# Clipping the attention scores on VectorE instead of GpSimd in a graph network kernel

## The chip, the cores and the metric

The kernel runs on one core of a Trainium2 chip. The metric is the time of one execution on the device in microseconds, the median of several runs. The core's engines are TensorE (PE in the profile), VectorE (DVE), ScalarE (ACT), GpSimd (POOL) and SyncE (SP), each with its own instruction stream; semaphores order them against each other.

## What is computed

Four graph layers over 6250 nodes of 96 features and 100000 edges sorted by destination. The change touches the first layer, an attention along the edges with four heads:

```python
q = (embeds[rows] @ qW).reshape(e, HEADS, dh)
k = (embeds[cols] @ kW).reshape(e, HEADS, dh)
v = (embeds[cols] @ vW).reshape(e, HEADS, dh)
scores = jnp.clip(jnp.einsum('ehd,ehd->eh', q, k), -10.0, 10.0)
exp_s = jnp.exp(scores)
norms = jax.ops.segment_sum(exp_s, rows, num_segments=nvar)[rows]
w = exp_s / (norms + 1e-08)
res = jax.ops.segment_sum(w[:, :, None] * v, rows, num_segments=nvar).reshape(nvar, d)
```

The other three (a softmax aggregation, ten steps of propagation, two graph convolutions) come behind it and are left as they are.

## The kernel before

Edges are first put in slots: one cell for each pair of a tile of 128 source nodes (49 tiles) and a group of 256 destination nodes (25 groups). The attention stage then goes over the source tiles, and within a tile over five **chunks** of five groups; a chunk holds 5 x 128 edge slots. There are 49 x 5 = 245 chunks. In the names below `X` is a pair of tiles and `e` a chunk in it.

No row is gathered by an address. VectorE builds one-hot matrices and TensorE multiplies by them. For a chunk:

- `turn_source` (L995) and `turn_destination` (L1000, twice) compare the slots' node numbers with the partition number: the one-hots `hT`, three planes of 640 in float16. TensorE uses them as weights to fetch the queries (`query`, L1117, into PSUM bank `pq`) and the keys and values (`take`, L1105, into banks `pk`). ScalarE copies the latter to SBUF in three pieces (`copy_kv`, L1180, into `kvs`).
- `score` (L981) multiplies queries, read from PSUM, by keys, and `score_sum` (L988) adds over the 24 features of a head: 128 x 20 scores `sc`.
- `clip` (L1057) bounds them by two values held per partition in `bound`.
- `exponent` (L1166, ScalarE) writes the exponentials into the weight columns of `wv`.
- `weigh` (L1062, GpSimd) multiplies the values by them, 128 x 480, also into `wv`.
- `total` (L1127, TensorE) sums `wv` by source node with the one-hots `hs` (`one_hots`, L1024, float32, 128 x 640).
- `one_hots` also makes `hd` (L1029, bfloat16, 128 x 768), by destination; `build` (L1141) multiplies it by `hs` to get the dense adjacency blocks that the later layers use, and `evacuate` (L1159) copies these out.

The order is written by hand. Each engine has a step function, called for c = 0, 1, 2, ...; within it each piece of work is for chunk c minus a fixed lag. On VectorE a step is `score` of chunk c-2, `turn_source` of c, `score_sum` of c-2, `turn_destination` of c, every fifth step `factors` (L1008 to L1019: a cast and three small products from which `hd` is made), `one_hots` of c, and once in five steps the reciprocal L1035. On GpSimd a step is `clip` and `weigh` of chunk c-2, and once in five steps `denominate` (L1071) or `normalize` (L1076 to L1080). On TensorE it is `take` and `query` of c-1, `build` of c-1 and `total` of c-3. On ScalarE it is `copy_kv` of c-1, once in five `copy_sums`, `exponent` of c-2, `evacuate` of c-1. The texts below name a step by c modulo 5: step 0 is the one with `factors`, step 4 the one that ends with the reciprocal.

Most buffers are double (`hT`, `kvs`, `qk`, `sc`, `wv`, `hd`), `rows` and `hs` have five.

## Time and profile before

| | |
|---|---|
| median of 3 runs | 4195.71 us (4194.11 to 4196.58) |
| profiled execution, own time | 4197.43 us |
| its span | 4196.1 us |
| mean granted TensorE clock | 0.981 |
| busy: TensorE, VectorE, ScalarE, GpSimd | 3913.7, 1912.2, 1301.4, 574.5 us |
| L1057, the clip on GpSimd, 245 of them | 251.2 us busy |
| L1062, `weigh`, 245 | 248.3 us busy |
| L1024, `hs`, 245 | 237.4 us busy |

The span is 4196.1 us, in which the attention stage lies between about 280 and 1235 us. A timeline row gives the start of an instruction from the span's start, its length, the engine, the line, the operation, what it writes and reads (with partitions x elements and type), and how many neighbouring ones the row merges. In brackets stands how long the engine had been idle and what ended that. Starts on VectorE can be closer than the lengths: the end of one instruction overlaps the start of the next.

### The profile page before, as it was taken

To read this page: it belongs to the slowest core of one execution; us is meant where nothing else is said; L and a number is where in the kernel's file an instruction comes from. 1 tells how busy PE (TensorE), PEld (TensorE's weight loads), DVE (VectorE), ACT (ScalarE), POOL (GpSimd) and SP (SyncE) were. 2 spreads that over 40 slices of the span, in tenths; PEclk is the share of its full clock that TensorE was granted. 3 is DMA by queue.
4 is the path that set the end of the run, shared out by engine and by line. 5 is a ranking of instruction groups with operands and counts; after the bars stand their busy time and mean duration, and the time that the engine had idled before them with its cause. 6 is when DMAs were issued, how large, how long until landed. Compare 5 with 4: busy or idle time off the path is not lost.

```text
span 4196.1 us, 126663 instructions
## 1 busy us (share of the span) xinstructions
PE 3913.7 (93%) x46212; PEld 3676.0 (88%) x46212; DVE 1912.2 (46%) x4409; ACT 1301.4 (31%) x4246; POOL 574.5 (14%) x708
## 2 busy tenths in 40 slices
PE   3779999999979999899999999999999999979898
PEld 2668999999965556899999999999999999979898
DVE  8989999999984332322222222222222222251211
ACT  1236666666653000222222222222222222220100
POOL 1015565555540000000000000000000000000000
PEclk9989999999989999999999999999999999989999
DMA  1029889898883331566665556666666565556574
GB/s 39 3 69 212 212 212 213 210 211 212 211 222 97 113 108 54 198 203 203 203 203 203 203 203 203 203 203 203 203 203 203 203 202 202 183 167 203 166 214 137
DMA packets 525172, 746.04 MB, mean 178 GB/s; under 512 B 203503, under 2 KB 449647, under 8 KB 525036
## 3 DMA queue, kind: packets, MB, share of 16 engines
q1 hardware_dynamic: 520040, 743.21, 59.8%
q8 instruction: 102, 1.67, 0.2%
q10 hardware_dynamic: 4996, 0.88, 0.1%
q14 instruction: 34, 0.28, 0.0%
HBM read 620.51 MB, written 83.32 MB: 168 GB/s over the span
## 4 chain that ended last, share of the span: by engine, by line
PE 70%; DVE 11%; issue 5%; SPq 5%; DMA 4%; POOL 2%; ACT 2%; DVEq 0%; ACTq 0%; POOLq 0%
PE sum L1580 47%; PE sum L1325 14%; PE sum3a L1325 4%; DMA rows<-slot_rows_d 4%; SPq L955 2%; DVE onerank L756 2%; POOL sc L1057 1%; PE pk L1105 1%; DVE sc L988 1%; DVE qk L981 1%; PE pr L1127 1%; SPq L962 1%; DVE hd L1029 1%; SPq L951 1%; DVE bt L728 1%
## 5 line engine op out<-in xcount | busy, mean ns | idle before, releaser
L1580 PE MATMUL sum<-y,ring 128*128 128x192 f16 x12005 | 994.9, 246 | 4.1 <-ACT y L1482 4.1
L1580 PEld LDWEIGHTS sum<-y,ring 128*128 128x128 fp8e4 x12005 | 993.7, 98 | 4.7 <-issue 4.3
L1580 PE MATMUL sum<-u2b,ring 128*128 128x192 f16 x12005 | 991.2, 246 | 0.0
L1580 PEld LDWEIGHTS sum<-u2b,ring 128*128 128x128 fp8e4 x12005 | 990.5, 98 | 0.0
L1325 PE MATMUL sum<-u,ring 128*128 128x385 f16 (+1 forms) x4802 | 614.4, 288 | 31.1 <-ACT u L1450 22.2
L1588 DVE TENSOR_TENSOR z<-lo,sum 128x96 f32<-128x96 f32 x490 | 124.7, 254 | 1119.6 <-ACT lo L1603 1119.1
L1325 PEld LDWEIGHTS sum<-u,ring 128*128 128x128 fp8e4 x4802 | 435.9, 98 | 200.0 <-issue 38.2
L1105 PE MATMUL pk<-kv,hT 128*128 128x192 f16 x4900 | 487.6, 247 | 14.7 <-DVE hT L1000 9.5
L1105 PEld LDWEIGHTS pk<-kv,hT 128*128 128x128 f16 x4900 | 408.2, 99 | 23.7 <-ACT kvs L1180 12.1
L1180 ACT ACTIVATE kvs<-pk 128x384 f32<-128x384 f32 x735 | 310.2, 436 | 248.1 <-PE pk L1105 191.4
L1603 ACT ACTIVATE lo<-sum 128x96 f32<-128x96 f32 x490 | 122.6, 250 | 747.3 <-PE sum L1580 747.3
L1127 PE MATMUL pr<-wv,hs 128*128 128x101 f32 x2450 | 322.7, 279 | 14.7 <-ACT sums L1187 13.5
L1057 POOL TENSOR_SCALAR sc<-sc,bound 128x20 f32<-128x20 f32 x245 | 251.2, 1025 | 499.0 <-DVE sc L988 498.5
L1127 PEld LDWEIGHTS pr<-wv,hs 128*128 128x128 f32 x2450 | 292.2, 191 | 23.4 <-ACT sums L1187 21.9
L1062 POOL TENSOR_TENSOR wv<-kvs,wv 128x480 f32<-128x480 f32 x245 | 248.3, 1013 | 109.6 <-ACT wv L1166 109.6
L1325 PE MATMUL sum3a<-u,ring 128*128 128x192 f16 x2401 | 212.4, 250 | 30.2 <-ACT u L1723 28.0
L1024 DVE TENSOR_TENSOR hs<-count,ss 128x640 f32<-128x640 bf16 x245 | 237.4, 969 | 0.0
L1325 PEld LDWEIGHTS sum3a<-u,ring 128*128 128x128 fp8e4 x2401 | 204.1, 100 | 35.6 <-issue 23.6
L1591 DVE SCALAR_TENSOR_TENSOR uf<-z,col_g,H 128x96 f32<-128x96 f32 x490 | 156.2, 319 | 90.0 <-DVE z L1588 90.0
L1159 ACT ACTIVATE row<-pc 128x512 uint16<-128x512 f32 (+1 forms) x343 | 186.9, 548 | 1.5 <-PE pc L1141 0.2
L1117 PE MATMUL pq<-q,hT 128*128 128x96 f16 x2450 | 145.0, 206 | 40.5 <-DVE qk L981 40.5
L1117 PEld LDWEIGHTS pq<-q,hT 128*128 128x128 f16 x2450 | 124.7, 98 | 51.2 <-issue 51.1
(248 smaller groups left out, 3097.0 us busy)
## 6 DMA issues: line engine op xcount, KB each, us to landing
ring<-adjacency_t SPq DMA_DIRECT2D x490, 800.0 KB, 4.3
ring<-adjacency SPq DMA_DIRECT2D x147, 896.0 KB, 4.8
rows<-slot_rows_d SPq DMA_DIRECT2D x245, 320.0 KB, 4.0
adjacency<-row SPq DMA_DIRECT2D x147, 128.0 KB, 3.5
adjacency_t<-col SPq DMA_DIRECT2D x147, 128.0 KB, 2.6
adjacency<-row SPq DMA_DIRECT2D x49, 256.0 KB, 3.5
adjacency_t<-col SPq DMA_DIRECT2D x49, 256.0 KB, 2.2
adjacency<-row SPq DMA_DIRECT2D x49, 160.0 KB, 3.9
```

The source lines that it names most:

```text
L1024: v.tensor_tensor(hs[h][:], under(k.count1[:], CHUNK), over(ss[b][:, 0, c, 0:CHUNK], P), ALU.is_equal).then_inc(k.hot.sem, 1)
L1057: pool.tensor_scalar(sc[i][:], sc[i][:], k.bound[:, 0:1], k.bound[:, 1:2], ALU.min, ALU.max).then_inc(k.clipped.sem, 1)
L1062: pool.tensor_tensor(wv[i][:, :, 0:D].rearrange("p g (h d) -> p g h d", d=DH), kv[i][:, :, D:2 * D].rearrange("p g (h d) -> p g h d", d=DH ...
L1105: t = pe.matmul(pk[(3 * e + n) % 2][:, place:place + 2 * D], hT[i][:, 1 + m, g * P:(g + 1) * P], k.kv[:, 2 * (g0 + g) + m, part, :], start ...
L1117: t = pe.matmul(pq[:, g * D:(g + 1) * D], hT[i][:, 0, g * P:(g + 1) * P], q2[b][:, part, :], start=part == 0, stop=part == 1)
L1127: t = pe.matmul(pr[:, 0:AV], hs[e % HOMES][:, g, :], wv[i][:, g, :], start=g0 + g == 0, stop=g0 + g == GROUPS - 1)
L1159: a.activation(flat(row[b][:, g:g + count, :]), pc[u % 2][:, 0:count * P], ACT.Copy, accum_out=rowsum[:, bass.ds(X * (2 * UP) + u, 1)]).th ...
L1180: a.activation(flat(kv[i][:, 2 * n:2 * n + count, :]), pk[(3 * e + n) % 2][:, 0:count * 2 * D], ACT.Copy).then_inc(k.kv_out.sem, 1)
L1325: t = pe.matmul(self.ps[j][:, 0:self.cols], w[:, q, (j + odd) // 2, :, (j + odd) % 2], self.U[:, r * RING + q, 0:self.cols], start=r == q ...
L1580: m = pe.matmul(ps[r][:, 0:2 * D], w[:, t // 2, :, t % 2], U[:, t, 0:2 * D], start=t == 0, stop=t == TILES - 1)
L1588: v.tensor_tensor(z[j][:], lo[j][:], ps[j][:, 0:D], ALU.add).then_inc(k.free.sem, 1)
L1591: v.scalar_tensor_tensor(uf[j][:], z[j][:], k.g[:, tile], flat(k.H[:, tile, :]), ALU.mult, ALU.add).then_inc(k.uf.sem, 1)
```

## The change

The clip moves from GpSimd to VectorE, with the same operation on the same operands, and is put between `turn_destination` and `factors` / `one_hots` of the step. Its lag of two chunks and its signal `clipped` to ScalarE stay. GpSimd's step then begins with `weigh`.

```diff
+    def clip(X, e):
+        i = e % 2
+        v.wait_ge(k.summed_qk.sem, k.summed_qk.at(X, e))
+        v.tensor_scalar(sc[i][:], sc[i][:], k.bound[:, 0:1], k.bound[:, 1:2], ALU.min, ALU.max).then_inc(k.clipped.sem, 1)
...
         for x, e in lagged(X, c, 0, first, chunks):
             turn_destination(x, e)
+        for x, e in lagged(X, c, 2, first, chunks):
+            clip(x, e)
+        for x, e in lagged(X, c, 0, first, chunks):
             if e % CHUNKS == 0:
                 factors(x, e)
             one_hots(x, e)
...
-    def clip(X, e):
-        i = e % 2
-        pool.wait_ge(k.summed_qk.sem, k.summed_qk.at(X, e))
-        k.settle(pool)
-        pool.tensor_scalar(sc[i][:], sc[i][:], k.bound[:, 0:1], k.bound[:, 1:2], ALU.min, ALU.max).then_inc(k.clipped.sem, 1)
...
     def gpsimd_step(X, c, first=False, chunks=CP):
         for x, e in lagged(X, c, 2, first, chunks):
-            clip(x, e)
             weigh(x, e)
```

VectorE, the step after the one with `factors` in the loop over tile pairs (step 1), before. A REGISTER_ALU row computes a semaphore's target value.

```order
L978 REGISTER_ALU x3
L980 REGISTER_ALU
L981 TENSOR_TENSOR qk<-pq,kvs 128x480
L995 TENSOR_SCALAR hT<-rows,pid 128x640
L988 TENSOR_REDUCE sc<-qk 128x20
L1000 TENSOR_SCALAR hT<-rows,dpid 128x640 x2
L1024 TENSOR_TENSOR hs<-count,ss 128x640
L1026 REGISTER_ALU
L1029 TENSOR_TENSOR hd<-high_d,low_d 128x768
```

The same place with the change (line numbers behind the new function are five higher there):

```order
L978 REGISTER_ALU x3
L980 REGISTER_ALU
L981 TENSOR_TENSOR qk<-pq,kvs 128x480
L1000 TENSOR_SCALAR hT<-rows,pid 128x640
L988 TENSOR_REDUCE sc<-qk 128x20
L1005 TENSOR_SCALAR hT<-rows,dpid 128x640 x2
L993 TENSOR_SCALAR sc<-sc,bound 128x20
L1029 TENSOR_TENSOR hs<-count,ss 128x640
L1031 REGISTER_ALU
L1034 TENSOR_TENSOR hd<-high_d,low_d 128x768
```

The clip, now L993, stands ahead of the two one-hots `hs` and `hd`; nothing else changed places.

GpSimd, three steps of the same loop before:

```order
L1057 TENSOR_SCALAR sc<-sc,bound 128x20
L1062 TENSOR_TENSOR wv<-kvs,wv 128x5x96
L1055 REGISTER_ALU
L1057 TENSOR_SCALAR sc<-sc,bound 128x20
L1062 TENSOR_TENSOR wv<-kvs,wv 128x5x96
L1055 REGISTER_ALU
L1057 TENSOR_SCALAR sc<-sc,bound 128x20
L1062 TENSOR_TENSOR wv<-kvs,wv 128x5x96
```

and with the change:

```order
L1064 TENSOR_TENSOR wv<-kvs,wv 128x5x96
L1063 REGISTER_ALU
L1064 TENSOR_TENSOR wv<-kvs,wv 128x5x96
L1063 REGISTER_ALU
L1064 TENSOR_TENSOR wv<-kvs,wv 128x5x96
```

One `weigh` a step is left there, with nothing ahead of it on its engine.

## Rows read from the trace of the kernel before

**Rows 1.** Busy time by engine in a stretch of the attention stage (columns ahead).
```profile
core 0: us, PE busy (x) PEld busy (x) DVE busy (x) ACT busy (x) POOL busy (x), PEclk, DMA share, GB/s
560.00:1230.00 670.00, 628.66 (x7794) 609.08 (x7792) 661.04 (x1381) 423.43 (x1250) 396.81 (x488) 1.00 0.90 211
```

**Rows 2.** Timeline, VectorE: start, length, instruction; L981 of six steps, 2 to 2.
```profile
1002.53 0.65 DVE L981 TENSOR_TENSOR qk<-pq,kvs 128x480 f32<-128x480 f32 x1
...
1006.10 0.65 DVE L981 TENSOR_TENSOR qk<-pq,kvs 128x480 f32<-128x480 f32 x1
...
1009.66 0.65 DVE L981 TENSOR_TENSOR qk<-pq,kvs 128x480 f32<-128x480 f32 x1
...
1013.31 0.62 DVE L981 TENSOR_TENSOR qk<-pq,kvs 128x480 f32<-128x480 f32 x1
...
1018.63 0.64 DVE L981 TENSOR_TENSOR qk<-pq,kvs 128x480 f32<-128x480 f32 x1
...
1021.85 0.65 DVE L981 TENSOR_TENSOR qk<-pq,kvs 128x480 f32<-128x480 f32 x1
```

**Rows 3.** Timeline, VectorE: what follows L981 in step 1.
```profile
1019.19 0.37 DVE L995 TENSOR_SCALAR hT<-rows,pid 128x640 f16<-128x640 f16 x1
1019.49 0.64 DVE L988 TENSOR_REDUCE sc<-qk 128x20 f32<-128x480 f32 x1
1020.05 0.67 DVE L1000 TENSOR_SCALAR hT<-rows,dpid 128x640 f16<-128x640 f16 x2
1020.64 0.81 DVE L1024 TENSOR_TENSOR hs<-count,ss 128x640 f32<-128x640 bf16 x1
1021.38 0.55 DVE L1029 TENSOR_TENSOR hd<-high_d,low_d 128x768 bf16<-128x768 bf16 x1
```

**Rows 4.** Timeline, GpSimd in steps 1 and 2, and VectorE's L995 of step 2.
```profile
1020.34 1.18 POOL L1057 TENSOR_SCALAR sc<-sc,bound 128x20 f32<-128x20 f32 x1 [2.79 <-DVE sc L988]
...
1021.94 1.00 POOL L1062 TENSOR_TENSOR wv<-kvs,wv 128x480 f32<-128x480 f32 x1 [0.43 <-ACT wv L1166]
...
1022.41 0.72 DVE L995 TENSOR_SCALAR hT<-rows,pid 128x640 f16<-128x640 f16 x1
```

**Rows 5.** Timeline, VectorE and GpSimd: step 0, and an earlier step 0.
```profile
1013.86 0.65 DVE L995 TENSOR_SCALAR hT<-rows,pid 128x640 f16<-128x640 f16 x1
...
1016.52 1.03 POOL L1062 TENSOR_TENSOR wv<-kvs,wv 128x480 f32<-128x480 f32 x1 [0.53 <-ACT wv L1166]
...
1016.61 1.63 DVE L1024 TENSOR_TENSOR hs<-count,ss 128x640 f32<-128x640 bf16 x1
...
299.12 0.28 DVE L1019 TENSOR_TENSOR high_d<-high_d,ss 128x240 bf16<-128x240 bf16 x1
...
299.13 1.13 POOL L1062 TENSOR_TENSOR wv<-kvs,wv 128x480 f32<-128x480 f32 x1 [0.51 <-ACT wv L1166]
...
299.32 1.62 DVE L1024 TENSOR_TENSOR hs<-count,ss 128x640 f32<-128x640 bf16 x1
```

**Rows 6.** Timeline, TensorE and ScalarE in step 1.
```profile
1019.40 0.60 PE L1117 MATMUL pq<-q,hT 128*128 128x96 f16 x10 [0.78 <-DVE qk L981]
...
1020.37 0.33 ACT L1180 ACTIVATE kvs<-pk 128x192 f32<-128x192 f32 x1 [1.22 <-PE pk L1105]
...
1021.55 0.31 ACT L1166 ACTIVATE wv<-sc,score_unit 128x20 f32<-128x20 f32 x1 [0.85 <-POOL sc L1057]
```

**Rows 7.** Instructions of one line: count, shortest/median/longest ns, first and last start.
```profile
L981 DVE TENSOR_TENSOR qk<-pq,kvs x245: 618/645/658, 285.7 to 1229.3; 128x480 f32<-128x480 f32 x123
...
L995 DVE TENSOR_SCALAR hT<-rows,pid x245: 368/654/721, 279.9 to 1223.3; 128x640 f16<-128x640 f16 x123
...
L1029 DVE TENSOR_TENSOR hd<-high_d,low_d x245: 543/548/559, 282.5 to 1225.6; 128x768 bf16<-128x768 bf16 x123
...
L295 DVE TENSOR_SCALAR col<-col x28: 170/172/911, 19.5 to 3735.8; 128x7 f32<-128x7 f32 x28
...
L1588 DVE TENSOR_TENSOR z<-lo,sum x490: 253/255/256, 1708.4 to 3685.2; 128x96 f32<-128x96 f32 x164
...
L1591 DVE SCALAR_TENSOR_TENSOR uf<-z,col_g,H x490: 317/319/322, 1708.9 to 3685.6; 128x96 f32<-128x96 f32 x164
```

## The prediction

> **What bounds the kernel now.** The change lies in the attention stage alone, so I read that stage first, by the busy time of each engine in a stretch of it [rows 1]. VectorE is busy 661.0 of 670 us (98.7%), TensorE 628.7 (93.8%), at a granted clock of 1.00; GpSimd 59%, ScalarE 63%. The page's totals (VectorE 46% of the span) hide this, since the later stages leave VectorE idle. Two engines are near their limit here, and VectorE is the nearer.
>
> Next the order of time on VectorE. A step begins with the product L981. Six such starts in a row [rows 2] give the steps 2, 3, 4, 0 and 1 (number of the step modulo five; step 0 builds the factors): 3.57, 3.56, 3.65, 5.32 and 3.22 us, 19.32 a block of five. The starts of L981 run from 285.7 to 1229.3 us [rows 7], 943.6 us, 48.8 such blocks. TensorE's share makes its own work 0.938 x 19.32 = 18.1 us a block, so it would become the bound if VectorE needed less than that. It waits for VectorE once a block, 0.78 us at the row shown [rows 6].
>
> What makes steps 1 and 2 differ is one instruction. In step 1 the comparison L995 takes 0.37 us [rows 3], in step 2 it takes 0.72 [rows 4]; the steps differ by the same 0.35. There GpSimd's `weigh` (L1062) runs from 1021.94 to 1022.94, over L981 and into L995, and L995 ends 0.19 after it (1023.13). L981, which reads one operand from PSUM, is not longer beside it (0.65 against 0.64 [rows 2]). So GpSimd and VectorE exclude each other in some instructions. The size of that is in step 0 [rows 5]: `weigh` starts at 1016.52, L1024 at 1016.61, and L1024 takes 1.63 us where it takes 0.81 otherwise [rows 3]. **A `weigh` that has the way holds such an instruction up for 0.82 us when it comes just before it.** L1024 ends at 1018.24, so it really began at 1017.43, 0.12 before `weigh`'s recorded end at 1017.55.
>
> Who wins when both want it? At 299.12 L1019 starts; `weigh` starts at 299.13 and takes 1.13 instead of 1.00, so it waited 0.13 for L1019; L1024 is issued right behind L1019 at 299.32 and takes 1.62 [rows 5]. `weigh`, waiting during one tensor_tensor, went ahead of the next one, although VectorE had no gap between them. A tensor_tensor and `weigh` thus exclude each other both ways, and the waiting GpSimd instruction goes at the border. In step 1 the clip points the same way: it starts at 1020.34 and ends at 1021.52, 0.14 after L1029's start at 1021.38 [rows 3, 4]: it got through at the border of L1024 and L1029, the very border at issue below.
>
> The Trainium skill (SBUF — State Buffer, Who interferes with whom) says that a VectorE instruction with two SBUF inputs, or in a mode with two ports, contends with a GpSimd one that reads SBUF, and that the one that issues first holds the shared pair for the whole instruction. The rows agree on who blocks, and show the release 0.12 us before the recorded end. Taken to the letter the rule would make each hold 0.12 longer, some 23 us on the sum below, as an estimate.
>
> **The removed clip.** GpSimd loses 245 clips, the one shown of 1.18 us [rows 4], most of it spent waiting behind L1024. GpSimd is not full, and the clip delayed nothing on VectorE that the rows show (L1029 took 0.55 behind it, as everywhere [rows 3, 7]). So its time is worth nothing by itself. What counts is that `clipped` is signalled at another moment.
>
> **The added clip.** It stands between the second L1000 and L1024, on the engine that is full, so all of its spacing is on the path. No row shows it; the nearest: a 128x7 tensor_scalar with two constants takes 172 ns (L295); a per-partition operand costs 319 - 255 = 64 ns (L1591 against L1588, both 128x96) [rows 7], and the clip has two: 300 ns. Back to back, instructions overlap: L1000 lasts 0.37 each, the pair 0.67 [rows 3], so 0.08 is hidden, and **0.22 us** a step is left. Bounds: 0.09 if both operands load unseen, 0.30 if nothing overlaps. I take 0.22, the sum of like rows. Its input, L988's result, is there over 0.5 us before [rows 3], so it waits for nothing.
>
> The Trainium skill (Perfetto Trace Analysis, Optimizing Scalar/DVE Operations) gives about 60 ns of overhead for a VectorE operation on SBUF, which would put the clip near 0.08 and the result 34 us below mine, as an estimate. The 300 ns above are from rows, and I stay with them.
>
> **Where `weigh` moves.** This is the larger part. Take a step whose L995 is free, as step 1 [rows 3], times from its L981 at 1018.63. The second L1000 starts at 1.72, the clip at 2.01 and ends at 2.31; L1024 is issued at 2.23 and L1029 is due at 2.97 (L1024's spacing is 1021.38 - 1020.64 = 0.74). The exponential starts 0.04 after the clip's end, as now (clip end 1021.52, L1166 at 1021.55; rounded up), lasts 0.31, and `weigh` starts 0.08 after that (L1166 ends 1021.86, `weigh` 1021.94) [rows 4, 6]: at 2.74. That is inside L1024, 0.23 before its border with L1029. `weigh` waits for it, goes first, and L1029 (also a tensor_tensor on two SBUF operands) is held for 0.82. ScalarE must be free at 2.35: its last copy of keys and values in that step ran from 1.74 to 2.07 (L1180 at 1020.37) [rows 6], so it is. Before, this exponential began at 2.92 and `weigh` at 3.31, after L1029 was through.
>
> In return `weigh` is over before the next L995, which gets its 0.35 back. The weights come 0.57 us earlier (less the wait); they feed the sum L1127 of the next step and free a buffer for L1180; neither is what VectorE waits for, so this earliness has no taker.
>
> **The sum**, for a block. A plain step is 3.22 + 0.22 + 0.82 = 4.26: steps 1, 2 and 3. Step 4 adds the reciprocal's 0.09 (3.65 - 3.56): 4.35. In step 0 the factors are built, and `weigh` falls among them or on L1024 as today; its 5.32 holds a late L995 of 0.65 for 0.37 (at 1013.86 [rows 5]), so 5.32 - 0.28 + 0.22 = 5.26. Together 3 x 4.26 + 4.35 + 5.26 = 22.39, that is +3.07 on 19.32. Times 48.8: **+150 us**. The profiled execution took 4197.4 (span 4196.1), 1.7 over the median 4195.7; from the median the sum gives **4346**. TensorE's 18.1 a block is far below 22.39, and the later stages are untouched.
>
> With the clip at 0.09 or 0.30 the result moves by 245 x 0.13 = 32 down or 245 x 0.08 = 20 up: 4314 to 4366.
>
> **Rivals.**
>
> A, *`weigh` comes behind L1029* (17%). My margin is 0.23 us less the time `weigh` needs from its start to its first read. If the exponential starts later, or VectorE keeps its turn at this border, `weigh` runs from L1029's end, beside L981 (not hindered), and holds L995, which wants to start 0.57 into the step, until 0.82: 0.25. Steps 2 and 3 are then 3.22 + 0.22 + 0.25 = 3.69, step 4 3.78, step 0 5.32 + 0.22 = 5.54, step 1 3.44: 20.14, +0.82 a block, +40: 4236. For it: the clip of today waited through all of L1024 although it had started before it (1020.34 against 1020.64 [rows 3, 4]). Against it: the border L1019/L1024 [rows 5].
>
> B, *L1029 is not held at all* (8%), the other side. None of the 245 L1029 took longer than 559 ns [rows 7], so no row shows it blocked; `weigh` never met it. Then a plain step is 3.44, a block 3 x 3.44 + 3.53 + 5.26 = 19.11, still over TensorE's 18.1: -10 us, 4186, and down to 4154 with the clip at 0.09. It decides if `weigh` can read beside L1029's bf16 operands. Against it: L1019 is of the same kind and type and did delay `weigh` [rows 5].
>
> C, *A with a cheap clip* (5%): at 0.09 a clip A's block is 20.14 - 5 x 0.13 = 19.49, +8 us, within 0.2% of 4196.
>
> **How the numbers follow.** Forecast 70%: 4346, by itself 4310 to 4366. The range must reach A to leave out no more than 2 in 10: 4215 to 4366. About 0.2% (8 us) is what a measurement of this kernel tells from no change. Slower by more: the forecast and A, 0.87. Faster by more: B, 0.08. Within: 0.05.
>
> **What would show it.** L1029's median rises from 0.55 to about 1.37 in four steps of five; L995's falls from 654 ns to 0.37; the clip's own row on VectorE reads about 0.30; `weigh` starts inside L1024 and its duration grows from 1.00 to about 1.2; plain steps are 4.26 apart; TensorE waits for L981 in every step. If L1029 stays at 0.55 and `weigh` starts after it, A holds; if it stays at 0.55 with `weigh` beside it, B. The forecast is wrong above all if `weigh` starts 0.2 us later than worked out.

## The result, and the profile after

| | before | after |
|---|---|---|
| median | 4195.81 us (4194.11 to 4196.61, 7 runs) | 4210.46 us (4208.70 to 4212.42, 7 runs) |
| ratio | 1 | 1.0035 [1.0023, 1.0047] |
| span of the profiled execution | 4196.1 us | 4209.5 us |
| mean granted TensorE clock | 0.981 | 0.981 |

The change costs 14.7 us. The forecast was 4346; the price of rival A was 4236. So the sign was right, the amount was not, and what the trace shows is rival A's mechanism at less than half its price (14.7 where A had 40).

In after the clip is L993, and the lines behind it have moved: `turn_source` is L1000 (L995 before), `turn_destination` L1005 (L1000), `hs` L1029 (L1024), `hd` L1034 (L1029), `weigh` L1064 (L1062), `exponent` L1167 (L1166). I name the work rather than the line below where both kernels are meant.

Busy time of each engine in the stretch of after that answers to [rows 1], with the same columns:

```profile
560.00:1230.00 670.00, 619.62 (x7665) 598.91 (x7665) 668.64 (x1533) 407.59 (x1227) 296.08 (x307) 1.00 0.87 208
```

VectorE is busy 99.8% of the stretch (98.7% before): it is still the bound, with 1533 instructions in the stretch where it had 1381. TensorE does less of its work per microsecond (619.6 against 628.7).

The starts of L981 in six steps of after, from the timeline of VectorE; they answer to [rows 2], steps 2, 3, 4, 0, 1 and the next 2:

```profile
678.79 0.65 DVE L981 TENSOR_TENSOR qk<-pq,kvs 128x480 f32<-128x480 f32 x1
...
682.39 0.64 DVE L981 TENSOR_TENSOR qk<-pq,kvs 128x480 f32<-128x480 f32 x1
...
685.99 0.65 DVE L981 TENSOR_TENSOR qk<-pq,kvs 128x480 f32<-128x480 f32 x1
...
689.68 0.62 DVE L981 TENSOR_TENSOR qk<-pq,kvs 128x480 f32<-128x480 f32 x1
...
695.04 0.65 DVE L981 TENSOR_TENSOR qk<-pq,kvs 128x480 f32<-128x480 f32 x1
...
698.45 0.65 DVE L981 TENSOR_TENSOR qk<-pq,kvs 128x480 f32<-128x480 f32 x1
```

The differences are 3.60, 3.60, 3.69, 5.36 and 3.41 us. Over the blocks of the stage behind its start (from 400 us on) the mean is 19.67 us a block, and that of before is 19.36 (the block that [rows 2] shows is 19.32). So +0.31 a block, and times 48.8 blocks that is 15 us: the whole result lies in the attention stage's steps, as the prediction said, but a step of four is 3.60 and not 4.26.

A step whose `turn_source` is free, step 1, in the timelines of VectorE, ScalarE and GpSimd of after; it answers to [rows 3, 4, 6]:

```profile
697.05 0.28 DVE L993 TENSOR_SCALAR sc<-sc,bound 128x20 f32<-128x20 f32 x1
697.25 0.81 DVE L1029 TENSOR_TENSOR hs<-count,ss 128x640 f32<-128x640 bf16 x1
697.98 0.55 DVE L1034 TENSOR_TENSOR hd<-high_d,low_d 128x768 bf16<-128x768 bf16 x1
...
697.37 0.31 ACT L1167 ACTIVATE wv<-sc,score_unit 128x20 f32<-128x20 f32 x1 [0.26 <-DVE sc L993]
...
697.75 1.64 POOL L1064 TENSOR_TENSOR wv<-kvs,wv 128x480 f32<-128x480 f32 x1 [3.98 <-ACT wv L1167]
```

Counted from that step's L981 at 695.04, the clip starts at 2.01 and ends at 2.29, `hs` starts at 2.21, `hd` at 2.94, the exponential at 2.33, `weigh` at 2.71. Forecast: 2.01, 2.31, 2.23, 2.97, 2.35, 2.74. `weigh` stands 0.23 before the border of `hs` and `hd` (the moment at which the one gives way to the other), just as forecast. Then comes the surprise. **`hd` starts on time and lasts 0.55.** `weigh`, which stood ready first, waits through `hs` and then through `hd` as well, and lasts 1.64 where it needs 1.00.

What it does in the step behind it, from the timelines of GpSimd and VectorE in after (steps 2 and 3); this answers to `weigh` and L995 in [rows 4]:

```profile
681.92 0.54 DVE L1034 TENSOR_TENSOR hd<-high_d,low_d 128x768 bf16<-128x768 bf16 x1
...
682.96 0.56 DVE L1000 TENSOR_SCALAR hT<-rows,pid 128x640 f16<-128x640 f16 x1
...
681.70 1.64 POOL L1064 TENSOR_TENSOR wv<-kvs,wv 128x480 f32<-128x480 f32 x1 [1.96 <-ACT wv L1167]
```

`weigh` ends at 683.34. Less its own 1.00 that is 682.34: it got its turn 0.12 before the recorded end of `hd` (682.46), beside L981, which it doesn't disturb. `turn_source` at 682.96 is held, but takes 0.56 and not the 0.72 of before. That is the reason why the loss is small: `weigh` waits at GpSimd's cost until `hd` is over, then works 0.14 earlier against the next step than before (0.05 before L981 at 682.39, where it was 0.09 behind L981 at 1021.85), and disturbs `turn_source` less.

Instructions of one line in after, count and shortest/median/longest ns; they answer to [rows 7], where `turn_source` had a median of 654 and `hd` a longest of 559:

```profile
L1000 DVE TENSOR_SCALAR hT<-rows,pid x245: 368/555/562, 280.0 to 1237.4; 128x640 f16<-128x640 f16 x123
...
L1034 DVE TENSOR_TENSOR hd<-high_d,low_d x245: 540/544/551, 282.6 to 1240.0; 128x768 bf16<-128x768 bf16 x123
...
L993 DVE TENSOR_SCALAR sc<-sc,bound x245: 279/283/294, 287.8 to 1244.8; 128x20 f32<-128x20 f32 x123
...
L1064 POOL TENSOR_TENSOR wv<-kvs,wv x245: 1003/1636/1643, 289.1 to 1245.5; 128x480 f32<-128x480 f32 x123
```

Not one of 245 `hd` was held: the longest is 551 ns. `weigh` met it in steps 1, 2 and 3 only, 146 times, each time having asked 0.22 to 0.23 before the border. In step 4 it asks too late to contend: ScalarE copies keys and values first (L1181 at 688.53), so the exponential starts 0.29 behind the clip's end, and `weigh` asks at 689.15, when `hd` has begun (689.13). And step 0 of after, which answers to [rows 5]:

```profile
690.23 0.49 DVE L1000 TENSOR_SCALAR hT<-rows,pid 128x640 f16<-128x640 f16 x1
...
692.67 1.10 POOL L1064 TENSOR_TENSOR wv<-kvs,wv 128x480 f32<-128x480 f32 x1 [0.89 <-ACT wv L1167]
...
692.83 1.08 DVE L1024 TENSOR_TENSOR high_d<-high_d,ss 128x240 bf16<-128x240 bf16 x1
```

Here L1024 (the last of the factors, 0.28 when free, as [rows 5] have it at 299.12) takes 1.08. `weigh` was ready at 692.67, waited 0.10 for the factor before, and went first at a border where VectorE had no gap. So both outcomes stand in one trace: GpSimd wins at a border among the factors in step 0, and loses at `hs`/`hd` in steps 1, 2 and 3.

**The books of a block** close with three items. The clip takes 0.20 of spacing in each of five steps: +1.00. `turn_source` is held 0.18 and no longer 0.35 in three steps, and 0.12 in place of 0.28 in step 0: -0.67 (3 x 0.17 + 0.16). Sum +0.33, against +0.31 measured, so that no other item of any size is missing.

### The profile page after: what moved, and what is told of

Read it like the earlier page. It is cut to its first block, busy times and chain, and to the rows that moved or that the text cites. A ratio compares the mean times of both kernels' runs of the same rounds, so it can differ in the third digit from the quotient of the medians.

```text
span 4209.5 us, 126418 instructions
## 1 busy us (share of the span) xinstructions
PE 3915.4 (93%) x46212; PEld 3675.9 (87%) x46212; DVE 1935.8 (46%) x4654; ACT 1290.2 (31%) x4246; POOL 438.6 (10%) x463
## 3 DMA queue, kind: packets, MB, share of 16 engines
q8 instruction: 100, 1.64, 0.2%
## 4 chain that ended last, share of the span: by engine, by line
PE 74%; DVE 16%; issue 5%; ACT 2%; DMA 1%; DVEq 1%; SPq 0%; ACTq 0%; POOL 0%; POOLq 0%
PE sum L1581 47%; PE sum L1326 14%; PE sum3a L1326 4%; PE pk L1106 3%; DVE qk L981 2%; PE pr L1128 2%; DVE sc L988 2%; DVE onerank L756 1%; DVE hT L1000 1%; DVE hd L1034 1%; PE pq L1118 1%; DVE sc L993 1%; DVE hs L1029 1%; DMA rows<-slot_rows_d 1%; DVE bt L728 1%
## 5 line engine op out<-in xcount | busy, mean ns | idle before, releaser
L1064 POOL TENSOR_TENSOR wv<-kvs,wv 128x480 f32<-128x480 f32 x245 | 362.4, 1479 | 758.6 <-ACT wv L1167 758.6
L1181 ACT ACTIVATE kvs<-pk 128x384 f32<-128x384 f32 x735 | 311.0, 437 | 367.5 <-PE pk L1106 300.3
L1029 DVE TENSOR_TENSOR hs<-count,ss 128x640 f32<-128x640 bf16 x245 | 198.7, 811 | 0.0
L1005 DVE TENSOR_SCALAR hT<-rows,dpid 128x640 f16<-128x640 f16 x490 | 167.6, 381 | 0.0
```

What stands on the lines that cost most here:

```text
L1005: t = v.tensor_scalar(hT[i][:, 1 + m, :], rows[h][:, 1, :], k.dpid[:, m:m + 1], None, ALU.is_equal)
L1029: v.tensor_tensor(hs[h][:], under(k.count1[:], CHUNK), over(ss[b][:, 0, c, 0:CHUNK], P), ALU.is_equal).then_inc(k.hot.sem, 1)
L1064: pool.tensor_tensor(wv[i][:, :, 0:D].rearrange("p g (h d) -> p g h d", d=DH), kv[i][:, :, D:2 * D].rearrange("p g (h d) -> p g h d", d=DH ...
L1181: a.activation(flat(kv[i][:, 2 * n:2 * n + count, :]), pk[(3 * e + n) % 2][:, 0:count * 2 * D], ACT.Copy).then_inc(k.kv_out.sem, 1)
```

## The experiments

All are edits of the kernel before or of the one after. Those of one batch share a chip, and each is compared with the kernel before on that chip. Where no ratio is given, the kernel was run once. Four kernels add rows of short **trials** behind the attention stage of the kernel before: in a trial VectorE does a clip-like operation, `hs`, `hd` and a reduction on buffers of their own, the clip's signal starts a copy on ScalarE, and its signal a product of 128 x 480 on GpSimd. The copy's length sets the moment at which GpSimd asks. Their total time is of no interest.

### When does GpSimd win: a matter of its moment, or of the kind of instruction?

84 trials: 16 delays of GpSimd's request for each of four chains (`hs`, `hd`; `hs`, `hs`; `hs`, a factor, `hd`; and the first with a one-input operation on GpSimd), ten for each of two others (`hd`, `hd`; two factors, `hs`). The clip of each trial stands behind a real wait.

```diff
+    for t, (x, n) in enumerate(trials):
+        v.wait_ge(pd.sem, pd.at(t))
+        v.wait_ge(vd.sem, vd.at(t))
+        v.tensor_scalar(p_sc[:], p_sc[:], p_bd[:, 0:1], p_bd[:, 1:2], ALU.min, ALU.max).then_inc(s1.sem, 1)
+        for op in kinds[x]:
+            op()
...
+        a.activation(p_out[:, 0:n], p_in[:, 0:n], ACT.Copy).then_inc(s2.sem, 1)
+        pool.wait_ge(s2.sem, s2.at(t + 1))
...
+            pool.tensor_tensor(p_w[:], p_v[:], p_in[:, 0:480], ALU.mult).then_inc(pd.sem, 1)
```

> The kernel before, with a section of 84 small trials put between the attention stage and the later layers; nothing else is changed. Each trial: VectorE issues the clip's operation, then a chain of tensor_tensor instructions back to back, then a reduction; the clip's signal goes to ScalarE (a copy of n elements, n sets the delay) and from there to GpSimd (a 128x480 product like weigh). Chains: A = hs then hd, B = hs then hs, C = hd then hd, D = 480 and 240 elements of bf16 then hs (the factor chain), E = hs, 240 elements of bf16, hd, F = as A but with a GpSimd tensor_scalar of one input. Theory T1 (time): GpSimd gets the pair at a border between two such instructions only if it starts less than about 0.2 us ahead of it. Then in A, B, C and E alike the second instruction grows by 0.82 us for starts within 0.2 of the border and not for earlier ones. Theory T2 (kind): VectorE keeps its turn from hs to hd whatever the time (A never grows), and D always grows. The whole adds some 300 to 450 us to the time.

Four rows of it, two trials of the chain `hs`,`hd`, one on each side of the border (GpSimd and VectorE):

```profile
1280.49 1.19 POOL L2141 TENSOR_TENSOR p_w<-p_v,p_in 128x480 f32<-128x480 f32 x1 [1.98 <-ACT p_out L2136]
1280.54 1.56 DVE L2115 TENSOR_TENSOR p_hd<-p_hi,p_lo 128x768 bf16<-128x768 bf16 x1
...
1284.07 1.64 POOL L2141 TENSOR_TENSOR p_w<-p_v,p_in 128x480 f32<-128x480 f32 x1 [2.39 <-ACT p_out L2136]
1284.10 0.55 DVE L2115 TENSOR_TENSOR p_hd<-p_hi,p_lo 128x768 bf16<-128x768 bf16 x1
```

A product that asked 0.05 us before the border went first and held `hd` for 1.00; one that asked 0.03 before didn't. In every chain GpSimd won in all trials in which it asked 0.05 or more ahead, and lost in all with 0.03 or less; of three at about 0.04 it won one. So the forecast's margin of 0.23 was ample, and neither the moment nor the kind of instruction explains the kernel after: the very pair `hs`,`hd` is held here and not there. This left the question of what else differs. The one-input operation held `hd` only to 0.94, that is 0.39, though it takes about 1.36 itself (a row of 1.66 with 0.30 of waiting in it).

### The moment again, in the kernel itself

One element on ScalarE ahead of the exponential of after makes `weigh` ask 0.1 later.

```diff
+        a.activation(pause[i][:, 0:PAUSE], k.ones[:, 0:PAUSE], ACT.Copy)
```

> The changed kernel with one more ScalarE instruction (one element a partition) between the clip's signal and the exponential, which makes weigh start some 0.1 us later: about 0.12 us ahead of the border of hs and hd in place of 0.23. T1 (time decides who gets the pair): hd is held for 0.82 us in three steps of five, some 2.5 us a block, about 4330 us. T2 (VectorE keeps its turn at this border): hd stays at 0.54, weigh gets 0.1 shorter and the time stays at 4210 within 5 us.

4212.09 us against 4199.13; `weigh` now asks 0.13 before the border in place of 0.23 and lasts 1.54, `hd` is as in after at 0.545, a block takes 19.67. This other moment within `hs` changes nothing.

### Is it the clip's place on VectorE, or only its time there?

The kernel before, with its clip on GpSimd, and a second clip on VectorE whose result nobody reads, at the place of the change:

```diff
+            v.tensor_scalar(scratch[e % 2][:], k.ones[:, 0:CHUNK * HEADS], k.bound[:, 0:1], k.bound[:, 1:2], ALU.min, ALU.max)
```

> The kernel before with a second, idle clip on VectorE at the place where the change puts it (reads ones and the bounds, writes a scratch tile that nobody reads); the real clip stays on GpSimd. Theory 'clip costs its spacing, weigh's earliness gives part back': the spacing of 0.20 us goes on every step and nothing comes back: 245 x 0.20 = 49, 4245 us. Rival 'the clip is cheap, the 15 us are waits': close to 4210.

4212.46 us, ratio 1.0032 [1.0020, 1.0045]: the same as after (1.0035), and not the 4245 that I expected. Timelines of VectorE and GpSimd in a step 2 of it (here the idle clip is L1047, the real one L1059, `weigh` L1064):

```profile
684.87 0.28 DVE L1047 TENSOR_SCALAR scratch<-ones,bound 128x20 f32<-128x20 f32 x1
685.07 0.81 DVE L1025 TENSOR_TENSOR hs<-count,ss 128x640 f32<-128x640 bf16 x1
...
684.57 0.52 POOL L1059 TENSOR_SCALAR sc<-sc,bound 128x20 f32<-128x20 f32 x1 [0.96 <-DVE sc L989]
685.57 1.65 POOL L1064 TENSOR_TENSOR wv<-kvs,wv 128x480 f32<-128x480 f32 x1 [0.48 <-ACT wv L1168]
```

GpSimd's clip, 1.18 long before [rows 4], is through in 0.52: it ends at 685.09, where `hs` begins. The idle instruction gave it a place to finish ahead of `hs`, so `weigh` asks as early as in after, and loses `hd` as in after (steps 3.60, 3.60, 3.69, 5.37, 3.42). **The cost is the extra VectorE instruction; which engine does the real clip makes no difference that these runs can tell.**

### The clip between `hs` and `hd`

After, with `one_hots` in two parts, so that `weigh` asks some 0.85 later in its step:

```diff
-        for x, e in lagged(X, c, 2, first, chunks):
-            clip(x, e)
...
-            one_hots(x, e)
+            one_hots(x, e, part=0)
+        for x, e in lagged(X, c, 2, first, chunks):
+            clip(x, e)
+        for x, e in lagged(X, c, 0, first, chunks):
+            one_hots(x, e, part=1)
```

> The changed kernel with the clip one place later, between hs and hd, so that weigh starts beside the next step's product and not inside hs. Theory 'earliness gives back': hs and hd are not touched, L995's stand-in (turn_source) is held some 0.29 us in place of 0.18, a plain step 3.71 for 3.60, a block about 20.1 for 19.67, 4231 us. Rival 'weigh's place gives nothing': 4210 as the changed kernel.

4211.30 us, ratio 1.0030 [1.0019, 1.0042]. In a plain step, VectorE's `turn_source` and GpSimd's `weigh` (L1071 here):

```profile
683.78 0.66 DVE L1000 TENSOR_SCALAR hT<-rows,pid 128x640 f16<-128x640 f16 x1
...
683.25 1.01 POOL L1071 TENSOR_TENSOR wv<-kvs,wv 128x480 f32<-128x480 f32 x1 [2.70 <-ACT wv L1174]
```

`weigh` waits for nothing (1.01) and holds `turn_source` by 0.29, the plain step is 3.71, both as forecast. But in the 4231 that I expected I had left step 0 as it was, and there `weigh` no longer meets the factors: 4.66 in place of 5.36. A block is 19.66 all the same, with quite other parts.

### What is `weigh` worth in all?

The kernel before without the multiplication of `weigh`; that part of the computation is left out, its signal is given at once (and `wv` is filled with ones once, at the start):

```diff
-        pool.tensor_tensor(wv[i][:, :, 0:D].rearrange("p g (h d) -> p g h d", d=DH),
...
-                           ALU.mult).then_inc(k.weighted.sem, 1)
+        pool.sem_inc(k.weighted.sem, 1)
```

> The kernel before without weigh's multiplication (GpSimd only signals; the values are not weighted, so the attention's result is not computed). It prices all of weigh's contention: VectorE needs 17.1 a block without it, TensorE 18.1. Theory 'contention is the slack that can be had': TensorE becomes the bound, a block 18.1 to 18.4, about 50 us below the kernel before. Rival 'VectorE's time is its own': no more than 10 us below.

4173.47 us against 4196.16: 23 us, not 50. The holds are gone, but a block still takes 18.89, since VectorE now waits, most of all in step 4, as a row of its timeline shows:

```profile
689.79 0.39 DVE L995 TENSOR_SCALAR hT<-rows,pid 128x640 f16<-128x640 f16 x1 [1.32 <-PE pk L1102]
```

The profile names TensorE's `take` (L1102) here, but the `take` that L995 must wait for is that of two chunks before, and its last matmuls had ended at 687.18. What L995 also waits for is the load of its own `rows` (L938, from DRAM, 4.1 us from issue to landing in the median). L995 waits more than 0.06 us in 125 of 245 chunks, and in every one of them its own load had landed 0.02 to 0.13 us before it started; the waits sum to 77 us, 1.58 a block. (The profile puts 91 of them down to this load and 22 to `take`.) So it is the loads of `rows` that keep this kernel at 18.9 a block, and not TensorE, which it never brought to its limit (614.6 of 640 us busy from 560 to 1200). The kernel before already waited so 37 times, for 14 us in all. Rival B's 4154 asks for a block of 18.5, below what this kernel reached with no product of `weigh` at all.

### The score's sum right behind its product

The kernel before, and then the one after, with `score_sum` moved to directly behind `score`, so that `weigh` runs beside two instructions that don't mind it, one with an operand from PSUM, the other a reduction with one input:

```diff
         for x, e in lagged(X, c, 2, first, chunks):
             score(x, e)
+            score_sum(x, e)
...
-        for x, e in lagged(X, c, 2, first, chunks):
-            score_sum(x, e)
```

> The kernel before (clip on GpSimd) with VectorE's sum L988 put directly behind its product L981 and turn_source after both, so that the first 1.2 us of a step need no shared pair and weigh, which starts 0.1 into the step, can finish there. Theory 'what bounds is the hold of turn_source': it goes, 0.35 a step, against 0.12 for the sum's wait on the product: a plain step 3.34, below TensorE's own 3.51; a block 18.6 to 18.8, about 33 us below the kernel before. Rival 'the hold moves to another instruction (an earlier weigh meets hs)': no gain, within 5 us of the kernel before or slower.

> The changed kernel with the same reordering. Its clip costs 0.20 a step on VectorE; weigh waits for the end of hd and then runs beside product and sum. Theory 'the 0.20 of the clip stays and the hold goes': a plain step 3.54, a block 19.5, about 4204, some 40 us above the reordered kernel with the clip on GpSimd. Rival 'hd is held now that the timing shifted': plain steps above 4.2, over 4300.

On before: 4198.53 us, ratio 1.0005 [0.9996, 1.0015]; the steps are 3.47, 3.35, 3.99, 5.16 and 3.40, 19.37 a block, as before. `turn_source` is free in four steps of five (in step 2 it is still held, by 0.13), but the gain is paid back: the sum waits for the product's result, 0.12 in each step, and L981 of step 0 waits some 0.30 for a copy of keys and values in 46 of 49 blocks. One step of it, step 3, VectorE's `hs` and `hd` and GpSimd's clip (L1056 here):

```profile
678.22 0.82 DVE L1024 TENSOR_TENSOR hs<-count,ss 128x640 f32<-128x640 bf16 x1
678.96 0.55 DVE L1029 TENSOR_TENSOR hd<-high_d,low_d 128x768 bf16<-128x768 bf16 x1
...
677.63 1.94 POOL L1056 TENSOR_SCALAR sc<-sc,bound 128x20 f32<-128x20 f32 x1 [0.61 <-DVE sc L988]
```

In steps 1 and 3 the clip now loses the border too and waits until `hd` is over (679.57), which moves `weigh` back. And step 0 of this kernel has the outcome that I had forecast for after, at the same border `hs`/`hd` and with the same `weigh` (L1061 here):

```profile
687.28 1.35 DVE L1029 TENSOR_TENSOR hd<-high_d,low_d 128x768 bf16<-128x768 bf16 x1
...
687.19 1.03 POOL L1061 TENSOR_TENSOR wv<-kvs,wv 128x480 f32<-128x480 f32 x1 [0.51 <-ACT wv L1165]
```

`weigh` asks 0.09 before the border and goes first: `hd` is held by 0.80, in step 0 of 48 blocks out of 49. It won in five plain steps too, in which it asked 0.17 to 0.41 ahead, 53 times of 53 in all.

On after: 4208.73 us, ratio 1.0029 [1.0017, 1.0041], where I expected 4204; steps of 3.54, and 5.37 for step 0, since `weigh` is clear of `turn_source` but not of the factors, and the sum now waits for the product's result (from L981 to the first `turn_destination` 1.54, 681.12 to 682.66, against 1.42 in step 1 of after, 695.04 to 696.46). Here `weigh` asks 0.17 to 0.22 before the border in 146 steps, and loses in all.

### What stands ahead of the clip

Trials again, now with a reduction ahead of each (so that the clip itself doesn't follow a wait), and further operations between:

```diff
+        v.wait_ge(pd.sem, pd.at(t))
+        v.wait_ge(vd.sem, vd.at(t))
+        red()
+        for op in ahead:
+            op()
+        v.tensor_scalar(p_sc[:], p_sc[:], p_bd[:, 0:1], p_bd[:, 1:2], ALU.min, ALU.max).then_inc(s1.sem, 1)
+        hs()
+        hd()
```

> Again trials between the attention stage and the later layers of the kernel before; now the chain clip, hs, hd gets, one by one, what the real step has and the first trials had not: K the broadcast operand of weigh, J semaphore waits and signals at hs and hd, G two float16 comparisons back to back ahead of the clip, H a product from PSUM, a comparison, a reduction and a comparison queued behind hd, I all of K, G and H, L all of I and J; A none. In the first trials GpSimd, waiting during hs, went ahead of hd every time and held it for 1.00 us. Theory 'ahead': an unbroken run of instructions that use the shared pair, begun before GpSimd asks, keeps it; hd is held in A, K, J, H and not in G, I, L. Theory 'behind': what is queued behind hd decides; H, I, L are not held. Theory 'signals': J and L are not held. Theory 'operand': K, I, L are not held.

`hd` took 1.55 with nothing more ahead, whether or not semaphores stood at `hs` and `hd`, and whatever came behind; 1.35 where the product's second operand was broadcast as `weigh`'s is (a hold of 0.80). With two comparisons like `turn_destination` ahead of the clip it took 0.55: GpSimd lost. **In these trials what VectorE has done before the border decides it**, not the pair at the border.

> Trials between the attention stage and the later layers of the kernel before. Each is a reduction, some instructions ahead, then clip, hs, hd; GpSimd's product asks for the pair during hs, with two delays each. Shown before: nothing ahead, hd is held 1.0; two float16 comparisons ahead, it is not. Here 16 sets ahead: none, 1, 2 and 3 float16 comparisons (float16 output, mode with two ports), 1 and 2 float16 products, 1 and 2 float32 products, 1 and 2 float32 comparisons, reductions in several places. Theory 'kind': only a 16-bit two-port instruction right ahead of the clip protects hd, one is enough, a reduction between it and the clip undoes it. Theory 'length': any unbroken run of pair-using instructions that is long enough protects it, so two products do too. Theory 'queue': any two further instructions ahead do, the reductions too.

The sets are those of the text above. Held: nothing more ahead; one float16 product; one float32 product; a product from PSUM and a reduction. Not held: one, two or three comparisons in float16; one or two in float32; two products of either type; two reductions; mixtures of comparisons and reductions.

### How long may the unbroken stretch be, and does a real wait end it?

The same with one to four operations of a kind, and with `gap`, a reduction whose signal VectorE waits for:

```diff
+        kinds = [(o,) * c for o, cs in ((red, (0, 1, 2, 3, 4)), (tt, (1, 2, 3, 4)), (tb, (1, 2, 3, 4)), (qk, (1, 2, 3)), (ti, (1, 2, 3, 4)), (td, (1, 2))) for c in cs]
+        kinds += [(gap,), (td, td, gap), (td, gap, td), (qk, red), (red, qk), (qk, qk, red), (tt, red), (red, tt)]
```

> Trials as before (a reduction, a set ahead, clip, hs, hd; GpSimd asks during hs, one delay), with sets of one kind in rising number: reductions 0 to 4, float32 products 1 to 4, float16 products 1 to 4, products from PSUM 1 to 3, 20-element tensor_scalars with a constant 1 to 4, comparisons 1 and 2; then sets in which the clip waits for the signal of the reduction just ahead of it, and mixed pairs. Theory 'count since the engine last waited': up to one instruction ahead hd is held, from two on it is not, whatever the kind, and a wait right ahead of the clip brings the hold back, as in the loop with the sum just ahead of the clip. Rival 'kind': the counts of reductions and of products from PSUM never protect. Rival 'time': what protects is the time since VectorE last waited (about 1 us), so four small tensor_scalars do not and two long products do.

Three of its trials: none more ahead, two reductions more, and two comparisons and then `gap` (VectorE's `hd`, GpSimd's product; for the third also what stands ahead of them, with the pause of 0.04 from 1342.58 to 1342.62):

```profile
1244.90 1.55 DVE L2126 TENSOR_TENSOR p_hd<-p_hi,p_lo 128x768 bf16<-128x768 bf16 x1
...
1244.85 1.20 POOL L2178 TENSOR_TENSOR p_w<-p_v,p_in 128x480 f32<-128x480 f32 x1 [7.96 <-ACT p_out L2176]
...
1254.02 0.55 DVE L2126 TENSOR_TENSOR p_hd<-p_hi,p_lo 128x768 bf16<-128x768 bf16 x1
...
1253.84 1.79 POOL L2178 TENSOR_TENSOR p_w<-p_v,p_in 128x480 f32<-128x480 f32 x1 [3.52 <-ACT p_out L2176]
...
1341.93 0.65 DVE L2138 TENSOR_REDUCE p_red<-p_v 128x20 f32<-128x480 f32 x1
1342.62 0.30 DVE L2171 TENSOR_SCALAR p_sc<-p_sc,p_bd 128x20 f32<-128x20 f32 x1
...
1343.56 1.55 DVE L2126 TENSOR_TENSOR p_hd<-p_hi,p_lo 128x768 bf16<-128x768 bf16 x1
...
1343.38 1.32 POOL L2178 TENSOR_TENSOR p_w<-p_v,p_in 128x480 f32<-128x480 f32 x1 [3.68 <-ACT p_out L2176]
```

Held: none or one reduction more; one float32 product; one, two and three products from PSUM; a PSUM product and a reduction in either order; all three sets with `gap`. Not held: two or more reductions, two or more float32 products, one to four float16 products, one to four small operations, one or two comparisons, and the other mixtures. A count doesn't explain this (three PSUM products held, one small operation not), nor does a time. And one float16 product ahead was held in the run before and not in this one, the same chain. So the exact rule stays open: there is a state in it that my trials don't control. One pair of trials differs in the pause alone: two comparisons and a reduction ahead lose GpSimd the border (in the run before), and with VectorE waiting for that reduction's signal GpSimd wins it. Nor do comparisons ahead lose it everywhere: in the kernel before with the sum behind its product, three of them stand directly ahead of `hs` in the plain steps, with a pause of 0.03 ahead of the reduction before them, and there `weigh` won all five times that it contended.

### The loss that I had forecast, brought about

If a pause is what counts, one just ahead of the clip must bring the forecast's 0.82 back in the kernel itself. After, with `score_sum` directly ahead of the clip, so that the clip really waits for its signal (the expectation, older than the trials with `gap`, had the reduction itself in mind, as an instruction that needs no shared pair):

```diff
-        for x, e in lagged(X, c, 2, first, chunks):
-            score_sum(x, e)
         for x, e in lagged(X, c, 0, first, chunks):
             turn_destination(x, e)
         for x, e in lagged(X, c, 2, first, chunks):
+            score_sum(x, e)
             clip(x, e)
```

> The changed kernel with the sum L988 moved from between the comparisons to just ahead of the clip, so that a reduction, which needs no shared pair, stands between the two float16 comparisons of turn_destination and the run of clip, hs and hd. Theory 'what stands right ahead of the clip protects hd': hd is now held by weigh for 0.8 us in four steps of five, plain steps 4.3, a block near 22, about 4320 us, the loss I had forecast. Rival (the real loop protects hd by something else): plain steps 3.7 (0.12 for the sum's signal), about 4230 us.

4354.76 us against 4198.31. VectorE and GpSimd in one step:

```profile
742.34 0.64 DVE L988 TENSOR_REDUCE sc<-qk 128x20 f32<-128x480 f32 x1
743.02 0.29 DVE L993 TENSOR_SCALAR sc<-sc,bound 128x20 f32<-128x20 f32 x1
743.23 0.82 DVE L1029 TENSOR_TENSOR hs<-count,ss 128x640 f32<-128x640 bf16 x1
743.96 1.36 DVE L1034 TENSOR_TENSOR hd<-high_d,low_d 128x768 bf16<-128x768 bf16 x1
...
743.74 1.17 POOL L1063 TENSOR_TENSOR wv<-kvs,wv 128x480 f32<-128x480 f32 x1 [3.19 <-ACT wv L1166]
```

The reduction ends at 742.98, the clip starts at 743.02. `weigh` asks 0.22 before the border, as in after (0.22 at 681.70), and this time goes first: `hd` lasts 1.36, held by 0.82. That is so in 170 of 245 steps; in two more `weigh` asked 0.02 or less before the border and lost. Plain steps are 4.21 to 4.35 in the mean, step 4 is 4.33, step 0 5.47, a block 22.62. The forecast had 4.26, 4.35, 5.26 and 22.39. The sum of the prediction was thus right for a kernel that differs from after by the place of one reduction and 0.04 us of pause. This kernel alone can't tell the two apart; the pair of trials above, in which the reduction stands in both, speaks for the pause.

### A kernel that uses this

After, with the sum behind its product, and the clip between `hs` and `hd`: `weigh` then starts when `hd` is over, and has only the product from PSUM and the reduction beside it (the two edits shown above, together).

> Product and sum adjacent at the start of VectorE's step (as in adj_after) and the clip on VectorE between hs and hd (as in late). weigh then starts at 0.05 in the next step, beside product and sum, and is done before turn_source at 1.26. Theory 'contention gone': plain step 3.54, step 0 near 4.5, VectorE 18.7 a block, so TensorE's chain bounds at about 18.9 (the block without weigh): some 22 us below the kernel before. Rival 'latency back on the chain': weigh's later end starves TensorE's sum, a block of 19.3 or more, no gain.

**4175.00 us, ratio to before 0.9941 [0.9927, 0.9955]**, faster than both kernels. A plain step on VectorE, with GpSimd's `weigh` behind it (L1070 here):

```profile
668.55 0.65 DVE L981 TENSOR_TENSOR qk<-pq,kvs 128x480 f32<-128x480 f32 x1
669.24 0.65 DVE L988 TENSOR_REDUCE sc<-qk 128x20 f32<-128x480 f32 x1
669.81 0.38 DVE L1000 TENSOR_SCALAR hT<-rows,pid 128x640 f16<-128x640 f16 x1
...
671.43 0.29 DVE L993 TENSOR_SCALAR sc<-sc,bound 128x20 f32<-128x20 f32 x1
671.63 0.55 DVE L1039 TENSOR_TENSOR hd<-high_d,low_d 128x768 bf16<-128x768 bf16 x1
...
668.60 1.00 POOL L1070 TENSOR_TENSOR wv<-kvs,wv 128x480 f32<-128x480 f32 x1 [2.54 <-ACT wv L1173]
```

`weigh` runs from 668.60 to 669.60, all of it beside L981 and the reduction. It takes 1.00 and holds nobody: `turn_source` starts at 669.81 and takes 0.38. Steps 3.55, 3.55, 3.66, 4.56, 3.54; a block 18.87, that is 0.49 less than before, times 48.8 24 us. Busy time of each engine in a stretch of it (columns as in [rows 1]):

```profile
560.00:1200.00 640.00, 611.62 (x7635) 595.77 (x7633) 632.31 (x1529) 413.41 (x1221) 206.56 (x304) 1.00 0.96 217
```

VectorE is busy 98.8% of it, so this kernel is bound by VectorE's own work, and not by TensorE as I had expected. The block adds up from that work: 19.36 less all holds (0.35 in three steps, 0.28 and 0.82 in step 0, together 2.15), with five clips (1.00) and five waits of the sum for the product (0.60), makes 18.81. That the kernel without `weigh`'s product stands at 18.89 is a coincidence: there VectorE is idle for 8% of the time, behind the loads of `rows`.

## Why the prediction was wrong

Point by point, by its steps:

- **VectorE is the bound, and all that is added to it counts.** Right: 98.7% busy before, 99.8% after, and the idle clip alone gave the whole loss. The 18.1 for TensorE was never put to the test: the first limit below VectorE's work, which the prediction doesn't have, was the loads of `rows`, at 18.89 a block.
- **The removed clip is worth nothing.** Right: the kernel that keeps it and adds an idle one takes the same time.
- **The added clip, 0.22.** Right in kind, and 0.02 too much: 283 ns long, 0.20 from its start to that of `hs`. Two rows of the trials with one to four operations ahead show what it is made of, an operation on 20 elements with a constant (L2154) and then the clip of the trial (L2171):

```profile
1316.40 0.17 DVE L2154 TENSOR_SCALAR p_t<-p_v 128x20 f32<-128x20 f32 x1
1316.48 0.29 DVE L2171 TENSOR_SCALAR p_sc<-p_sc,p_bd 128x20 f32<-128x20 f32 x1
```

  The one with a constant has a spacing of 0.08 and is 0.12 shorter than the clip; the clip has two per-partition operands and a second operation more, and 0.06 for each operand is what the prediction had from L1591 and L1588. The Trainium skill's 60 ns of overhead (Perfetto Trace Analysis, Optimizing Scalar/DVE Operations), from which I had worked out a clip near 0.08 as an estimate, agrees with the operation with a constant; as an estimate for the clip it failed, since it left out the two operands: the clip's spacing is 0.20.
- **`weigh` asks at 2.74, inside `hs`.** Right for the step worked out: 2.71, each term before it met within 0.03, and the same 0.23 before the border in steps 2 and 3. In step 4 it is not so: ScalarE isn't free, and `weigh` asks 0.02 behind the start of `hd`.
- **The waiting GpSimd instruction goes at the border.** This is the step that failed, and with it the 0.82 for a held `hd` in four steps of five. I read it from the factors and L1024 [rows 5] and applied it to `hs` and `hd`, where it lost all 146 times: `hd` took 0.54 to 0.55, and `weigh` waited for it. The rule was right at its own place, and is so in after (692.67 and 692.83). But the factors stand behind a cast whose signal VectorE really waits for, with a pause of 0.04 (in after the cast L1013 at 692.08 ends at 692.27, the first factor starts at 692.31), while in a plain step VectorE makes no pause that the trace shows, and `hs`/`hd` stand at the end of it. That a pause can turn the border is shown by the trials with two comparisons and a reduction, with and without `gap`, and the kernel with the reduction ahead of the clip agrees. Step 0 of the kernel before with the sum behind its product points the same way: behind the factors' pause `weigh` wins at `hs`/`hd` itself, in all 48 blocks in which it asked there. That the pause is the whole difference between the factors and `hs`/`hd` is inferred from this, not tried apart, and what decides a border with no pause close ahead stays open.
- **The clip as a witness for this.** I wrote that the clip of before "got through at the border of L1024 and L1029, the very border at issue". It did end there, with no pause ahead, and without making `hd` longer (0.55); whether it went ahead of `hd` or beside it the rows don't tell, and nothing that I have now explains it. In the kernel with the sum behind the product, the same clip lost that border in two steps of five. One witness that agreed with the forecast was thus of another kind: 20 elements of one input, asking before `hs` began. The same rows also spoke the other way, since the clip had lost the border in front of `hs`; I had seen that, and gave rival A only 17% for it.
- **The size of a hold, 0.82.** Right where it occurs: the median `hd` of the kernel with the pause takes 1359 ns, against 544 in after, 0.815.
- **Rival A, 4236.** Right mechanism, two of its terms mis-sized. It let `turn_source` begin 0.82 into the step, held by 0.25; it began at 0.76 (683.52 - 0.37 = 683.15, less 682.39), held by 0.19, in the medians 0.18. That is 0.19 before `weigh`'s recorded end, where `hs` had been released 0.12 before; [rows 3, 4] already had it for the comparison (1023.13 - 0.37 = 1022.76, 0.18 before `weigh`'s end at 1022.94). And it left step 0 with L995's old hold of 0.28; `weigh` of step 4 comes earlier in that step too, and the hold is 0.12. With the clip's 0.02 in each, the first makes 0.09 less in steps 2, 3 and 4, the second 0.18 less in step 0, and step 1 has 0.02 less: 0.27 + 0.18 + 0.02 = 0.47, which takes A's 20.14 to the measured 19.67.
- **The range.** 4215 to 4366 reached rival A with 21 us to spare below its price. A hold of 0.18 for 0.25 in three steps and of 0.12 for 0.28 in step 0 already makes 0.37 a block or 18 us, and the clip 5 more: the result lies 4.5 us below the range.

The Trainium skill (SBUF — State Buffer, Who interferes with whom) says that a VectorE instruction with two SBUF inputs contends with a GpSimd one that reads SBUF, that the pair of ports they share is an exclusive lock, and that the order of issue decides who blocks. Blocking is as it says: `weigh` gets nowhere through `hs`. By the order of issue `weigh`, ready at 681.70, would go before `hd`, issued at 681.92. The trace has `hd` first, in all 146 cases in which `weigh` had asked before it, and the measurement decides: a waiting GpSimd instruction can be passed by the next of VectorE's, and whether it is depends on what went before.

## What to carry to other kernels

Moving work from an engine with time to spare to the one that is full costs its full spacing, and here that was all: 0.20 us in each of 245 steps, less what a neighbour gave back. Where two engines share a resource, read who wins at the very border in question. A border elsewhere, even between instructions of the same kind, may go the other way: with one reduction moved, and a pause of 0.04 us ahead of the border, the kernel lost some 140 us (156 over before, where after is 15 over). What helped was not to win or lose the border but to have no quarrel: put GpSimd's SBUF work beside VectorE's instructions that it doesn't hold, here a product from PSUM and a reduction (0.65 each beside it). The price was 0.12 a step for the sum's wait, and 23 us were left as gain. And before a second kernel's equal time is taken for a common floor, look at what each waits for: one block of 18.9 was VectorE's own work, the other the loads of `rows`.

## What was unexpected of the hardware

- The same two instructions, `hs` and `hd`, with GpSimd asking 0.2 us before their border: `hd` at 0.54 to 0.55 in all 146 such steps of one kernel, at 1.36 in 170 steps of the other.
- In the trials in which GpSimd could win, it had to ask some 0.04 us before the border: it won at 0.05 and more, lost at 0.03 and less, and went either way between.
- The hold depends on GpSimd's operands: 1.00 for a product of two full inputs, 0.80 to 0.82 with a broadcast second input, 0.39 for an operation with one input (which itself takes about 1.36), at the same 128 x 480 elements.
- On 20 elements a VectorE operation with a constant has a spacing of 0.08 us, the clip with its two per-partition operands 0.20: by this an operand costs some 0.06, nearly as much as the rest of the operation.
- An idle instruction of 20 elements on VectorE let GpSimd's clip through ahead of `hs`: its length fell from 1.17 to 0.52 us in the median.
- Left open: which state of VectorE decides the border in an unbroken stretch. Chains of equal count and of equal length went both ways, and one and the same chain did so in two kernels.
